# Attention in ten units a head instead of twelve, with the row maxima one unit earlier

## What is computed

```python
att = einsum('bhgqd,bhkd->bhgqk', qg, k) / sqrt(D_HEAD)
att = where(causal, att, -inf)
probs = softmax(att, axis=-1)
ctx = einsum('bhgqk,bhkd->bhgqd', probs, v)
x = x + ctx.reshape(...) @ Wo
```

## Time and profile before

| what | value |
|---|---|
| median of 3 runs | 1605.55 us (1603.5 to 1607.41) |
| the profiled execution | 1605.24 us, its span 1603.5 us |
| PE, DVE, ACT, POOL busy over the span | 97%, 59%, 37%, 39% |
| attention in the span | about 555 to 1188 us |
| one head in its steady part | 36.77 us |

### The profile page before, as it was taken

The page is one execution under the profiler, slowest core; times in us unless marked ns, Lnnn a source line. Parts: engine busy times, 40 slices in busy tenths (PEclk is TensorE's granted clock), DMA queues, the critical chain, the costliest instruction groups (busy, mean ns, idle before and its releaser), DMA issues. The chain is left out here.

```text
span 1603.5 us, 26749 instructions
## 1 busy us (share of the span) xinstructions
PE 1551.8 (97%) x9440; PEld 1199.6 (75%) x9440; DVE 938.3 (59%) x2707; ACT 587.7 (37%) x1201; POOL 621.0 (39%) x403
## 2 busy tenths in 40 slices
PE   7999998999999789999999999999999999999999
PEld 7999998788888655555555555555468999999998
DVE  6544563646463387888888878887527333333333
ACT  4323323212120126666666656666633111111110
POOL 1322223434343306676777666667742011010100
PEclk8999999999999969999999999999999999999999
DMA  6332233333322444443333334342344131323221
GB/s 226 121 122 94 107 134 132 119 119 118 105 93 79 131 96 97 103 96 87 87 87 94 94 91 96 97 109 62 87 170 147 53 105 53 106 64 93 78 66 40
DMA packets 152312, 162.77 MB, mean 102 GB/s; under 512 B 41744, under 2 KB 110608, under 8 KB 151920
## 3 DMA queue, kind: packets, MB, share of 16 engines
q1 hardware_dynamic: 123600, 137.37, 29.7%
q10 hardware_dynamic: 28592, 23.86, 4.5%
HBM read 104.05 MB, written 61.90 MB: 103 GB/s over the span
## 5 line engine op out<-in xcount | busy, mean ns | idle before, releaser
L1479 ACT ACTIVATE at_probs<-ps 128x512 f32<-128x512 f32 (+3 forms) x768 | 324.0, 494 | 141.0 <-PE ps L1395 138.6
L1552 DVE CUSTOM_DVE_ANT_0 ps<-ps,at_score_mask 128x512 f32<-128x512 f32 (+3 forms) x512 | 290.8, 618 | 37.6 <-PE ps L1384 34.7
L1395 PE MATMUL ps<-at_qs,at_ks 98*128 98x512 f32 (+3 forms) x528 | 192.7, 391 | 8.4 <-ACT at_probs L1479 6.0
L328 POOL TENSOR_TENSOR f_x_ring<-f_x_ring,f_half_bias 128x1024 f32<-128x1024 f32 x32 | 77.3, 2416 | 312.9 <-DVE f_h L582 312.4
L1384 PE MATMUL ps<-at_ks,at_qs 96*128 96x512 f32 (+3 forms) x528 | 175.6, 368 | 11.7 <-DMA at_ks<-scr_k_hi 11.1
L1395 PEld LDWEIGHTS ps<-at_qs,at_ks 98*128 98x128 f32 x528 | 97.4, 193 | 116.8 <-ACT at_probs L1479 91.5
L1410 PE MATMUL ps<-at_probs,at_vs 128*32 128x512 f32 (+3 forms) x1536 | 162.7, 496 | 0.2 <-POOL at_probs L1308 0.2
L1330 POOL TENSOR_TENSOR at_added<-at_added,at_probs 128x2048 f32<-128x2048 f32 x32 | 148.2, 4631 | 2.3
L1552 DVE CUSTOM_DVE_ANT_0 ps<-ps,at_score_mask,at_part_max 128x128 f32<-128x128 f32 (+3 forms) x256 | 134.1, 557 | 13.0 <-issue 10.6
L48 PE MATMUL f_ps<-f_wt_hi,f_hT_hi 128*128 128x400 f32 (+1 forms) x384 | 134.2, 350 | 3.2 <-DVE f_hT_lo L586 3.2
L1308 POOL TENSOR_SCALAR_AFFINE_SELECT at_probs<-at_probs 128x512 f32<-128x512 f32 x128 | 82.1, 652 | 137.9 <-ACT at_probs L1479 137.9
(11 more groups left out here) (159 smaller groups left out, 3158.3 us busy)
## 6 DMA issues: line engine op xcount, KB each, us to landing
at_qs<-scr_q_hi SPq DMA_DIRECT2D x20, 512.0 KB, 6.4
f_x_ring<-in_L_attn_resid SPq DMA_DIRECT2D x16, 512.0 KB, 3.6
x<-f_x_ring SPq DMA_DIRECT2D x16, 512.0 KB, 2.7
early<-x SPq DMA_DIRECT2D x16, 512.0 KB, 3.3
scr_q_hi<-qkv_rope_hi ACTq DMA_DIRECT2D x32, 256.0 KB, 2.0
scr_q_lo<-qkv_rope_lo ACTq DMA_DIRECT2D x32, 256.0 KB, 2.3
scr_ctx_hi<-at_ctx_hi SPq DMA_DIRECT2D x32, 256.0 KB, 2.2
scr_ctx_lo<-at_ctx_lo SPq DMA_DIRECT2D x32, 256.0 KB, 2.5
```

The lines of the kernel that those rows point to most:

```text
L328: pool.tensor_tensor(x_ring[:, u, :], x_ring[:, u, :], half_bias[:], ALU.add).then_inc(bias_added, 1)
L1395: pe.matmul(score_ps[(u * G + g) % BANKS][:, 0:z - a], ks[:, nm, j * P:(j + 1) * P], qs[nm][0:KROWS + 2, half, g, a - half * HALF:z - half ...
L1479: act.activation(probs[:, u % PROBS, g, 0:z - a], score_ps[(u * G + g) % BANKS][:, 0:z - a], ACT.Exp, scale=SCALE).then_inc(exp_done, 1)
L1552: dve.tensor_tensor_reduce(out=src, in0=src, in1=mask, scale=1.0, scalar=part_max[:, g, own] if c else -3.0e38, op0=ALU.add, op1=ALU.max, ...
```

## The change

Key blocks 2 and 3 of half 0 become one unit, and blocks 6 and 7 of half 1 another. A head has 10 units, of widths 512, 384, 384 (256 + 128) in half 0 and five times 512, 384, 384 (256 + 128) in half 1. A merged unit has two score matmuls for each g, into the same bank one behind the other, with one exponential over both; one mask instruction for its two triangles; and its products and sums are still made block by block. The ring of `probs` is now counted through all heads, because 10 is no multiple of 6. The items of head m are dealt over ten units as before over twelve, but the stretch begins one unit earlier, in the last unit of head m-2, and turn B of head m-1 goes into that same unit. The places of the steps of a half move: `high(n, 0)` on ACT from unit 10 (of 0 to 11) to unit 9 (of 0 to 9), `divide(n, 0)` on POOL from 9 to 8, `low(n, 0)` from 11 to 9, and others with them. The list of SP stays as it was. At the very end each half of the first output projection waits for its own sum to be read, and only the last turn waits for all slots.

```diff
-    ADDED = range(4, 8)
+    ADDED = range(3, 7)
...
-        units = [(half, j) for half in range(2) for j in range(QH * (half + 1))]
+        units = [(0, (0,)), (0, (1,)), (0, (2, 3))] + [(1, (j,)) for j in range(NQ - 2)] + [(1, (NQ - 2, NQ - 1))]
         NU = len(units)
-        LAST = {QH - 1: 0, NU - 1: 1}
+        H0 = QH - 1
+        LAST = {H0 - 1: 0, NU - 1: 1}
...
+        for m in range(2, NG + 1):
+            windows = [(m - 2, NU - 1)] + [(m - 1, u) for u in range(NU - 1)]
+            for at, items in zip(windows, spread(first, weight, [room[u] for _, u in windows])):
+                placed[at] = of(m, items) if m < NG else []
+            lead = placed[m - 2, NU - 1]
+            lead.insert(min(SLOTS, len(lead)), (m - 1, TURN_B))
...
             def mask(n, u):
-                tile = probs[:, u % PROBS, :, 0:P]
+                count = len(units[u][1])
+                tile = probs[:, (NU * n + u) % PROBS, :, :].rearrange("p g (b n) -> p g b n", b=2)[:, :, 0:count, 0:P]
...
-                    if u in (3, 4, 6):
-                        add(n, (5, 6, None, 7)[u - 3])
-                    if n and u == (9 if n == NG - 1 else 8):
+                    if u in (2, 3, 5):
+                        add(n, (4, 5, None, 6)[u - 2])
+                    if n and u == 7:
                         low(n - 1, 1)
+                    if u == 8:
+                        divide(n, 0)
+                    if u == 7:
+                        low_wo(n)
                     if u == 9:
-                        divide(n, 0)
-                    if u == (9 if n == NG - 1 else 8):
-                        low_wo(n)
-                    if u == 11:
                         low(n, 0)
...
             def scores(n, u, g):
...
+                for j, at, cols in blocks(u):
+                    last = pe.matmul(score_ps[x % BANKS][:, cols], ks[:, nm, j * P:(j + 1) * P], qs[nm][0:KROWS + 2, half, g, at],
+                                     start=True, stop=True)
+                last.then_inc(scores_done, 1)
...
             def products(n, u):
...
+                for j, at, cols in blocks(u):
+                    for g in range(G):
+                        last = pe.matmul(ctx_ps[g * DH:(g + 1) * DH, at], vs[:, n % RING, j, :],
+                                         probs[:, (NU * n + u) % PROBS, g, cols], start=j == 0, stop=u in LAST and j == js[-1])
...
                     if u in LAST:
                         copy_chunk(n, LAST[u])
-                    if n and u == 5:
+                    if n and u == 4:
                         high(n - 1, 1)
-                    if u == 7:
+                    if u == 6:
                         high_wo(n)
-                    if u == 10:
+                    if u == 9:
                         high(n, 0)
...
-                    if u == 5:
+                    if u == 4:
                         reciprocal(n, 0)
```

More of the change, by code:

```diff
@@ L1129, in attention_stage, with blocks, width @@
         ctx_stored = [sem(f"ctx_stored{h}") for h in range(2)]
-        units = [(half, j) for half in range(2) for j in range(QH * (half + 1))]
+        units = [(0, (0,)), (0, (1,)), (0, (2, 3))] + [(1, (j,)) for j in range(NQ - 2)] + [(1, (NQ - 2, NQ - 1))]
         NU = len(units)
-        LAST = {QH - 1: 0, NU - 1: 1}
[L1134 to L1142, removed]
+        H0 = QH - 1
+        LAST = {H0 - 1: 0, NU - 1: 1}
+        LAST_OF = (H0 - 1, NU - 1)
+        APART = (range(H0), range(ADDED[-1] + 1, NU))
+        def blocks(u):
+            half, js = units[u]
+            out, at = [], 0
+            for j in js:
+                a = max(j * P - half * HALF, 0)
+                out.append((j, slice(a, HALF), slice(at, at + HALF - a)))
+                at += HALF - a
+            return out
+        def width(u):
+            return blocks(u)[-1][2].stop
+        diagonal = [u for u in range(NU) if units[u][1][0] >= units[u][0] * QH]
         rows = [("row", i, g, c) for i in range(NQ) for c in range(i // QH + 1) for g in range(G)]
@@ L1154, in attention_stage @@
         weight = [row_keys(it[1], it[3]) + 800 if it[0] == "row" else 900 for it in first]
-        room = [queries(u)[1] - queries(u)[0] + 1200 for u in range(NU)]
+        room = [width(u) + 1200 for u in range(NU)]
         def spread(items, weights, spaces):
@@ L1183, in attention_stage @@
         early = rows[OPEN + 8:OPEN + 20]
[L1184 to L1191, removed]
+        for u in range(H0):
+            placed[0, u] = of(0, early[4 * u:4 * u + 4])
+        for u, items in enumerate(spread([TURN_A] + rows[at_a:], weight[at_a:], room[H0:NU - 1])):
+            placed[0, H0 + u] = of(1, items)
+        for m in range(2, NG + 1):
[3 more added lines that the diff above has]
+            lead = placed[m - 2, NU - 1]
+            assert len(lead) >= SLOTS or m == NG
+            lead.insert(min(SLOTS, len(lead)), (m - 1, TURN_B))
+        placed[NG - 1, NU - 1] = []
         for n in range(NG):
@@ L1199, in attention_stage @@
             for u in range(NU):
-                if n == 0 and u in (0, QH):
-                    for key in BEFORE[u // QH] + [key for part in BETWEEN[u // QH] for key in part]:
+                if n == 0 and u in (0, H0):
+                    for key in BEFORE[u // H0] + [key for part in BETWEEN[u // H0] for key in part]:
                         number[key] = len(number)
@@ L1406, in products @@
                     pe.wait_ge(exp_done, NU * G * n + (G * (u + 1) + BANKS))
[L1407 removed]
+                if js[0] == 0:
                     pe.wait_ge(ctx_copied, 2 * n + (half + 1))
[L1409 to L1411 removed]
+                for j, at, cols in blocks(u):
+                    for g in range(G):
+                        last = pe.matmul(ctx_ps[g * DH:(g + 1) * DH, at], vs[:, n % RING, j, :],
+                                         probs[:, (NU * n + u) % PROBS, g, cols], start=j == 0, stop=u in LAST and j == js[-1])
                 last.then_inc(unit_done, 1)
@@ L1424, in sums @@
                 for u in APART[half]:
[L1425 to L1428, removed]
+                    for j, at, cols in blocks(u):
+                        for g in range(G):
+                            last = pe.matmul(out[g * DH:(g + 1) * DH, at], ones[:], probs[:, (NU * n + u) % PROBS, g, cols],
+                                             start=u == 0, stop=u in LAST and j == units[u][1][-1])
                 last.then_inc(slot_filled, 1)
@@ L1433, in _ @@
                 for u in range(NU):
-                    if n == 0 and u in (0, QH):
-                        half = u // QH
+                    if n == 0 and u in (0, H0):
+                        half = u // H0
                         for m, it in BEFORE[half]:
@@ L1455, in _ @@
             for half in range(2):
-                if half:
-                    pe.wait_ge(slot_read, len(number) + SLOTS)
+                pe.wait_ge(slot_read, number[NG - 1, ("sum", half)] + (SLOTS + 1))
                 cols = slice(half * HALF, (half + 1) * HALF)
@@ L1471, in exps @@
             def exps(n, u, g):
[L1472 to L1475, removed]
+                x, cols = NU * G * n + (u * G + g), slice(0, width(u))
+                if g == 0 and NU * n + u >= PROBS:
+                    m, v = divmod(NU * n + u - PROBS, NU)
+                    act.wait_ge(unit_done, NU * m + (NU + 1 + (v if v in ADDED else LAST_OF[units[v][0]])))
                     if v in ADDED:
-                        act.wait_ge(added_done, ADDS * n + (ADDS * earlier + max(v - ADDED[0], 1)))
-                act.wait_ge(scores_done, NU * G * n + (u * G + g + 1))
-                act.activation(probs[:, u % PROBS, g, 0:z - a], score_ps[(u * G + g) % BANKS][:, 0:z - a], ACT.Exp,
+                        act.wait_ge(added_done, ADDS * m + (ADDS + max(v - ADDED[0], 1)))
+                act.wait_ge(scores_done, x + 1)
+                act.activation(probs[:, (NU * n + u) % PROBS, g, cols], score_ps[x % BANKS][:, cols], ACT.Exp,
                                scale=SCALE).then_inc(exp_done, 1)
             def copy_chunk(n, half):
-                act.wait_ge(unit_done, NU * n + (NU + (QH, NU)[half]))
+                act.wait_ge(unit_done, NU * n + (NU + LAST_OF[half] + 1))
                 act.wait_ge(clo_done, 2 * n + (half + 1))
@@ L1567, in _ @@
                 for u in range(NU):
-                    if n == 0 and u in (0, QH):
-                        for m, it in BEFORE[u // QH]:
+                    if n == 0 and u in (0, H0):
+                        for m, it in BEFORE[u // H0]:
                             slot_item(m, it)
-                        for items in BETWEEN[u // QH]:
+                        for items in BETWEEN[u // H0]:
                             for m, it in items:
```

31 lines of the change are left out of this document (13 added, 18 removed).

## The result

The changed kernel takes 1671.97 us (median of 4 runs, 1669.61 to 1673.17) against 1606.48 of the kernel before beside it: a ratio of 1.0409, with a 95% interval of 1.0394 to 1.0425. It is slower, as forecast, but by 65 us where 36 were forecast, and outside the range.

What follows compares the result with a forecast made beforehand. PE, busy 97% of the span, was taken to bound the kernel. 1605.2 us plus 24 for 14 longer heads (1.7 each) plus 12 for the clock gave 1641 us, range 1610 to 1662.

Steps and rivals of the forecast that it cites:

- The chain: From unit 0's first score through copy, `high`, `low`, store and small DMAs to half 1's first score: 6.07 to 6.6 us.
- Both links: `high` behind the copy on ACT, and turn B's small DMAs behind `store(n, 0)` on SP; together they delay PE.
- Unit 0: First unit of a head, alone covering the wait: 3.45 us, with ACT's exponentials of unit 2 0.54 later behind `high`.
- The clock: PE's granted clock falling behind each wait: 0.8 us a head, 12 us over 15 heads, bounds nothing and 25.
- the rival of 1654: The clock falls in every head: 15 x 1.7 = 25 us on top of 24, 1654 us; chance 0.26.
- Units 1 to 9: Remaining units of a steady head: 32.1 us, bounds 31.25 and 32.6.
- the paces: PE's two rates in a unit, its own instruction list or the return of a score bank: 31.25 us for units 1 to 9.
- 0.85 for DVE: Items waiting for DVE's slots: 0.55 us behind turn A in unit 3, 0.15 each in units 5 and 9.
- the faster rival's 1588: `high` runs ahead of the copy, PE never waits at unit 1: a head takes 35.55 us, 1588 in all; chance 0.08.
- the wait: PE standing still at the start of unit 1 for turn B's row maxima, about 2.9 us in every head.
- The ends: Heads 0 and 15 outside the 14 steady periods, booked together at nothing, within 3 us.
- the unchanged case: The wait gives back what PE otherwise loses, as DVE and ACT empty their queues: about 1603 us; chance 0.05.

Runs made afterwards that it cites:

- the two runs that cut one each: Changed kernel with `high(n, 0)` ahead of `copy_chunk` on ACT: 1598.4 us; changed kernel with `load_rows(n+1, 1)` ahead of `store(n, 0)` on SP: 1603.79 us.
- the chain mended: Changed kernel with `high(n, 0)` moved ahead of `copy_chunk` in unit 9 on ACT: 1598.4 us, 0.9949 to the kernel before.
- The shorter maxima: Changed kernel, `high` ahead of the copy, with DVE's row maxima over half their columns and no causal triangle: 1579.03 us, 0.9819 to the kernel before.

## Why the prediction was right in its sign and wrong in its size

**The chain was right, step by step.** Predicted from the first score of unit 0: copy at 0.14, `high` at 0.63, `low` at 1.34, the first store 0.02 after it, the second small DMA at 4.18, the score at 6.07 to 6.6. Measured: 0.13, 0.63, 1.33, 2.63, 4.24 and 6.13. The middle value taken, 6.35, allowed for stores ahead of the small DMAs on the queue; in 10 of the 15 heads they cost nothing. In four they did: in two of these SP took 1.45 and 1.59 us to issue the second store instead of 0.51, in two the second small DMA landed later, and PE waited 0.4 to 1.3 us longer. Unit 0 was put at 3.45 and took 3.46 (its products start at 880.80 and take 1.00). Both links are shown by the two runs that cut one each.

**The clock was mis-sized.** The step "0.8 a head, half of the 1.7: 12 us" halved a price that had to be paid in full: in the records of the granted clock every one of the 15 waits has a stretch at 1.2 GHz behind it, as with 0.64 over 884.92 to 888.40. The run that keeps PE at work puts it at 22 us, 1.5 a head and near the upper bound of 25. The rows had only 2.70 (fell) and 1.05 us (did not); 2.60 lay next to the first, and half was chosen with no row for it. That 2.70 was all that the trace has between 1.05 and 3 us, as the prediction says, is not so. Near the start of the kernel before, PE had been at work at the full clock, stood idle for 1.94 us, and the clock fell:

```profile
36.94 0.33 PE L391 MATMUL f_ps<-ident,f_low_s 128*128 128x128 f32 x1 [1.94 <-DVE f_low_s L612]
```

```profile
25.00:35.00 10.00, 9.99 (x57) 9.66 (x55) 7.33 (x11) 2.82 (x4) 5.36 (x2) 1.00 0.71 257
36.94:41.00 4.06, 4.06 (x14) 4.03 (x15) 2.28 (x11) 3.34 (x5) 0.00 (x0) 0.58 0.01 2
```

By the prediction's own way of counting that is 4.06 x 0.42 = 1.7 us once more, behind a shorter wait and with PE at work right up to it. It speaks for the full 1.7, and so for the rival of 1654. The Trainium skill's page TensorE: Matmul & The Clock Gate (HAM oscillation — how this bites in real kernels) describes a loop that falls back in every turn behind a DMA wait of about 3 to 5 us. The trace shows the same for waits from 2.57 us, shorter than in that loop.

**Units 1 to 9 were mis-sized, DVE's hold above all.** For units 1 to 9 the paces gave 31.25 us and 0.85 for DVE, 32.1. With the chain mended, from 889.70 to the next head's first score at 923.02, they take 33.3: 2.1 above the paces and 1.2 above the forecast, which is 17 us over 14 heads. Unit 3 was right (3.45 for 3.40); unit 5 takes 3.71 where 3.30 was charged, units 2, 7 and 9 some 0.2 more each. The shorter maxima give back 1.05 of it, and 0.58 of that in unit 5: there DVE holds PE by four times the 0.15 charged. In units 2, 7 and 9 together 0.6 us above the paces stay even then, so that part is not the maxima on DVE, and no run shows what it is. The upper bound was too low as well: twice the 0.85 gives 32.95, not 32.6. And the faster rival's 1588 kept the 3.45 for unit 0, which has the 0.54 for `high` in it; with `high` ahead of the copy unit 0 takes 2.95. So the same layout without the wait came out at 1598, with one term 0.5 too high and the other 1.2 too low.

**The ends were not nothing.** Head 15, booked with head 0 "at nothing, within 3 us", takes 35.45 us where it took 29.82: its wait is 3.01 us, and the clock over the 36 us from 1208 is 0.86. With PE kept at work through the wait it takes 32.18, so more than half of the 5.6 us is the clock.

In sum: 24 + 12 + 0 was forecast. By the runs it is 46 for the wait, 22 for the clock and 5 for the later exponentials, less 8 for the layout without the wait (1598.4 against 1606.5): 65 us. Of the 24, the wait and the units were netted: 41 for the wait (14 heads at 2.9) less 17 for the units were forecast there. The wait was near enough; the units gave back too little and the clock took too much. Of the 29 or 30 us that the forecast is short, some 17 are the units and 10 the clock; less 3 for a chain shorter than its middle value, the rest are the four longer waits and the ends.

**The rivals.** "It falls in every head", 1654, was the nearest and had 0.26. Neither the faster nor the unchanged case came about; that "faster" hung on the place of `high` in ACT's list was right, and the run that moves it there is the proof.

## What to carry to other kernels

When a step is renumbered, look at what stands ahead of it in its own engine's list at the new place: here a step that had run during the sums came to stand behind a copy that waits for what follows them, and three in-order lists carried that to a fourth. Where two transfers share one issuing queue, the one that the busiest engine waits for goes first. And waits of TensorE like these, of 2.6 us and more, are to be priced with the clock that falls behind them in full, here about half on top of the waits themselves (22 us on 46).

## What the runs showed of the chip that was not expected

The granted clock fell after shorter idle times than the kernel before had shown: 1.26 and 1.82 us of a waiting PE in one run, 1.65 and 1.87 in another, while 0.54 did not bring it down, nor 1.05 in rows 7 and 8. Between these the length of the wait did not settle it: behind 1.29 us in the first of these runs and behind one of 1.64 in the second the clock stayed full, behind another of 1.64 it fell. Matmuls whose results are thrown away kept it up and paid for themselves: 22 us.

SP's issue of the same 256 KB store took 0.51 us in most heads and from 0.7 to 1.8 in some, and the DMAs queued behind it went out as much later. Nothing here tells why.
